# A state-space layer and a top-2 expert layer on one core: expert weights fetched for each slot from DRAM, residual rows in sixteen transfers, blank rows moved ahead of the expert regions

## The reference

```
logits = xf @ Wr + br; top 2 of 16 experts, softmax weights
for each expert e:  h = silu(xf @ W1[e]) * (xf @ W3[e]);  y = h @ W2[e]
                    y = layernorm(y) * gamma[e] + beta[e];  out += weight * y
x = x + layernorm(out)
```

## Time and profile before

| | us |
|---|---|
| median of 3 runs (lowest, highest) | 968.94 (967.91, 969.12) |
| the profiled execution's own time | 968.34 |
| its span in the trace | 966.5 |
| PE busy | 933.1 (97%) |
| DVE, ACT, POOL busy | 724.8, 688.3, 621.8 |
| DMA moved | 75.25 MB |

### The profile page before, as it was taken

The page is one execution under the profiler, slowest core; times in us unless marked ns, Lnnn a source line. Parts: engine busy times, 40 slices in busy tenths (PEclk is TensorE's granted clock), DMA queues, the critical chain, the costliest instruction groups (busy, mean ns, idle before and its releaser), DMA issues.

```text
span 966.5 us, 26600 instructions
## 1 busy us (share of the span) xinstructions
PE 933.1 (97%) x7177; PEld 826.0 (85%) x7177; DVE 724.8 (75%) x2524; ACT 688.3 (71%) x1355; POOL 621.8 (64%) x814
## 2 busy tenths in 40 slices
PE   7999999999999999998959999999999999999995
PEld 4777877888878877887949999999999999999962
DVE  2379999999999998898823777677677677777747
ACT  3777787777788787775215778777777777877626
POOL 2445677777777777775661666666666666576647
PEclk9999999999999999999979999999999999999998
DMA  4001322121111111101786211111111111121076
GB/s 137 12 12 34 93 95 84 58 73 54 56 57 50 56 40 42 40 23 42 263 311 192 69 50 49 46 52 51 44 50 50 45 50 47 45 53 49 19 274 248
DMA packets 52255, 75.25 MB, mean 78 GB/s; under 512 B 11103, under 2 KB 30689, under 8 KB 51472
## 3 DMA queue, kind: packets, MB, share of 16 engines
q1 hardware_dynamic: 41632, 54.61, 18.4%
q0 software_dynamic: 8672, 16.93, 5.2%
q10 hardware_dynamic: 1808, 2.02, 0.7%
HBM read 47.09 MB, written 27.41 MB: 77 GB/s over the span
## 4 chain that ended last, share of the span: by engine, by line
PE 79%; DVE 8%; POOL 6%; issue 5%; DMA 1%; ACT 1%; POOLq 0%; DVEq 0%; SPq 0%; ACTq 0%
PE pA L2106 11%; PE pR L2106 11%; PE pA L1665 11%; PE pB L2114 6%; PE pY L2114 5%; PE pY L1779 4%; PE pB L1691 3%; PE pB L1825 3%; PE pA L1680 3%; PE pY L1815 3%; POOL chosen_scratch L698 2%; PE pY L1798 2%; PE pY L1747 2%; PE pA L1636 2%; PE pR L1763 2%
## 5 line engine op out<-in xcount | busy, mean ns | idle before, releaser
L698 POOL DMA_INDIRECT chosen_scratch<-yo,got_id x143 | 148.2, 1036 | 93.7 <-issue 87.9
L1026 ACT ACTIVATE stage<-w_sb 128x1024 f32 x143 | 151.3, 1058 | 56.6 <-issue 56.5
L1545 DVE TENSOR_TENSOR hidT<-pR,sil 128x512 f32<-128x512 f32 x143 | 98.9, 692 | 80.1 <-ACT sil L1021 59.2
L612 POOL DMA_INDIRECT slots_scratch<-xrow,send_at x128 | 134.6, 1052 | 34.1 <-issue 31.2
L2106 PE MATMUL pA<-xsT,stage 128*128 128x128 f32 x1144 | 151.3, 275 | 0.4 <-ACT xsT L1010 0.4
L2106 PE MATMUL pR<-xsT,stage 128*128 128x128 f32 x1144 | 151.1, 275 | 0.0
L2106 PEld LDWEIGHTS pA<-xsT,stage 128*128 128x128 f32 x1144 | 139.2, 192 | 0.7 <-ACT xsT L1010 0.6
L2106 PEld LDWEIGHTS pR<-xsT,stage 128*128 128x128 f32 x1144 | 139.0, 192 | 0.0
L1665 PE MATMUL pA<-xn,taps 128*128 128x512 f32 x256 | 129.8, 593 | 1.0 <-ACT xn L763 1.0
L688 POOL TENSOR_TENSOR ers<-eve,neg_half 128x1 f32<-128x1 f32 x143 | 81.5, 570 | 57.3 <-DVE eve L1557 32.2
L1021 ACT ACTIVATE sil<-pA 128x512 f32<-128x512 f32 x143 | 85.3, 596 | 25.3 <-PE pA L2106 15.3
(11 more groups left out here) (233 smaller groups left out, 2099.1 us busy)
## 6 DMA issues: line engine op xcount, KB each, us to landing
got<-slots_scratch SPq DMA_DIRECT2D x143, 65.0 KB, 1.8
w_sb<-chosen_scratch SPq DMA_DIRECT2D x16, 512.0 KB, 5.4
w_sb<-in_w_dram SPq DMA_DIRECT2D x1, 6144.0 KB
xin<-in_x_dram SPq DMA_DIRECT2D x16, 256.0 KB
xr<-in_x_dram SPq DMA_DIRECT2D x16, 256.0 KB
x_scratch<-x SPq DMA_DIRECT2D x16, 256.0 KB
w_sb<-in_w_dram SPq DMA_DIRECT2D x4, 1024.0 KB, 8.2
fx<-x_scratch SPq DMA_DIRECT2D x1, 4096.0 KB
```

The source lines that it names most:

```text
L612: eng.indirect_dma_start(slots_d, bass.IndirectOffsetOnAxis(ap=send_at[:, s % 2, k, t:t + 1], axis=0), xrow[:, s % 2, k, t, :], None).then ...
L698: eng.indirect_dma_start(chosen_d, bass.IndirectOffsetOnAxis(ap=got_id[:, j % NGOT:j % NGOT + 1], axis=0), yo[:, q, :], None, bounds_check ...
L1026: eng.activation(stage[:, j % NSTAGE, :, :].rearrange("p k f -> p (k f)"), w13_sb[:, bass.ds(e, 1), :, :].rearrange("p o k f -> p (o k f)" ...
L1545: eng.tensor_tensor(hidT[:, p, :], pR[:, p, :], sil[:, p, :], ALU.mult).then_inc(hid_ready, 1)
```

## The change

- `w13_sb` is no longer filled with weights. SP fetches each slot's 512 KB from DRAM straight into one of the four buffers `stage` (`load_weights`: a register load of the expert's number, a wait for `h3_mm` from slot 4 on, the DMA). The order on SP is slot rows and weights in turn for slots 0 to 3, then the rows of slots 4 to 7, and from then on in each turn n first the weights of slot n-4, then the waits for slot n-8, then the rows of slot n. ACT's `put_weights` is gone.
- Each region now begins with 128 blank rows, written for all 16 regions by one DMA of 1 MB early in stage 1; the tokens' rows start behind them. The tails are gone, with `tail_at`. The first row of a slot is the smaller of its place in the count and 128 rows before the region's end. So the last tile of a region may read rows that the tile before has read as well, or blank rows ahead of the region.
- Two stores that follow each other can therefore write the same rows of `chosen_scratch`; POOL waits before each store until the one before it has landed.
- DVE's table chain has more operations.
- The first layer's result comes back in 16 loads of 256 KB, one in every fourth slot from slot 16 on, and not in one of 4 MB.

```diff
@@ sync @@
-            def load_early():
-                eng.wait_ge(taps_ready, 1)
-                eng.wait_ge(xb_ready, NS)
-                eng.wait_ge(cv_mm, 2 * NS)
-                eng.wait_ge(in_mm, 2 * NS)
-                load_w13(0, 4)
             def load_late():
                 eng.wait_ge(y_step, 11 * NS)
-                load_w13(4, NE)
                 for k, v in enumerate((gamma, beta)):
...
             load_x(5)
+            eng.dma_start(slots_d[0:BLANK, :].rearrange("(e r) d -> e r d", e=NE)[:, 0:P, :].rearrange("e (p r) d -> p e (r d)", r=8),
+                          blank[:, :].rearrange("p (o f) -> p o f", o=1).broadcast_to([P // 8, NE, 8 * ROW])).then_inc(blank_stored, 16)
...
-            load_early()
             store_x1(14)
             load_late()
             store_x1(15)
-            eng.wait_ge(tail_ready, 1)
-            for e in range(0, NE, 2):
-                store_tail(eng, e)
...
-            eng.wait_ge(tails_stored, 16 * NE)
-            eng.wait_ge(blank_stored, 16)
+            eng.wait_ge(blank_stored, 32)
...
+            def load_weights(j):
+                e = eng.value_load(slot_table[0:1, j:j + 1], min_val=0, max_val=NE - 1)
+                wait_past(eng, h3_mm, j - NSTAGE + 1)
+                eng.dma_start(stage[:, j % NSTAGE, :, :], w13[:, bass.ds(e, 1), :, :].rearrange("p o k f -> p (o k) f")).then_inc(staged[j % NSTAGE], 16)
             for j in range(NGOT):
                 load_slots(j)
-            eng.dma_start(fx1[:, :, :, :], x1_d.rearrange("(g p t) d -> p g t d", p=P, t=NT4)).then_inc(fx1_loaded, 16)
-            for n in range(NGOT, NSLOT):
+                if j < NSTAGE:
+                    load_weights(j)
+            for n in range(NGOT, NSLOT + NGOT - NSTAGE):
+                load_weights(n - NGOT + NSTAGE)
+                if n >= NSLOT:
+                    continue
+                if n % 4 == 0 and 4 <= n // 4 < 4 + NG:
+                    g = n // 4 - 4
+                    eng.dma_start(fx1[:, g, :, :], x1_d[g * NT4 * P:(g + 1) * NT4 * P, :].rearrange("(p t) d -> p t d", t=NT4)).then_inc(fx1_loaded, 16)
                 eng.wait_ge(erw_ready, n - NGOT + 1)
                 eng.wait_ge(id_ready, n - NGOT + 1)
                 eng.wait_ge(wb_ready, n - NGOT + 1)
@@ gpsimd, store @@
                 eng.wait_ge(yo_ready, j + 1)
                 eng.wait_ge(id_ready, j + 1)
+                if j:
+                    eng.wait_ge(stored[(j - 1) % 4], ((j - 1) // 4 + 1) * 16)
@@ scalar @@
-            eng.wait_ge(tail_ready, 1)
-            for e in range(1, NE, 2):
-                store_tail(eng, e)
...
-            def put_weights(j):
...
-                if j + 2 < NSLOT:
-                    put_weights(j + 2)
@@ vector, once at the start @@
+                eng.tensor_scalar(running[:, :], running[:, :], float(P), None, ALU.add).then_inc(lower_ready, 1)
@@ vector, positions and the table @@
-                if s == NS - 1:
-                    eng.wait_ge(rank_read, NS)
-                    eng.tensor_scalar(tail_at[:, :], running[:, :], slot_no[:, 0:1], None, ALU.add).then_inc(tail_ready, 1)
...
-            r.step(eng.tensor_scalar(count_i[:, :], count_i[:, :], P - 1, None, ALU.add))
+            r.link(eng.memset(end_step[:, NE - 1:NE], float(BLANK + P)))
+            r.step(eng.tensor_tensor(end_step[:, 0:NE - 1], running[:, 1:NE], running[:, 0:NE - 1], ALU.subtract))
+            r.link(eng.tensor_tensor(end_step[:, NE - 1:NE], end_step[:, NE - 1:NE], running[:, NE - 1:NE], ALU.subtract))
+            r.step(eng.tensor_scalar(count_i[:, :], count_i[:, :], -1, None, ALU.add))
...
+            r.link(eng.tensor_tensor(past_end[:, :, :], past[:, :, :], end_step[:, :].rearrange("p (o e) -> p o e", o=1).broadcast_to([P, 2, NE]), ALU.mult))
             r.link(eng.tensor_reduce(slot_cols[:, 0:2], past[:, :, :], AX.X, ALU.add))
             r.step(eng.tensor_reduce(slot_cols[:, 2:4], past_step[:, :, :], AX.X, ALU.add))
+            r.link(eng.tensor_reduce(slot_end[:, :], past_end[:, :, :], AX.X, ALU.add))
...
-            eng.tensor_scalar(slot_cols[:, 2:4], slot_cols[:, 2:4], float(BLANK), None, ALU.min).then_inc(cols_ready, 1)
+            r.step(eng.tensor_scalar(slot_end[:, :], slot_end[:, :], running[:, 0:1], None, ALU.add))
+            r.step(eng.scalar_tensor_tensor(out=slot_cols[:, 2:4], in0=slot_cols[:, 2:4], scalar=float(2 * P), in1=slot_end[:, :], op0=ALU.add, op1=ALU.min))
+            eng.tensor_scalar(slot_cols[:, 2:4], slot_cols[:, 2:4], float(-P), None, ALU.add).then_inc(cols_ready, 1)
@@ tensor, up @@
-                    eng.wait_ge(staged, j + 1)
+                    eng.wait_ge(staged[j % NSTAGE], j // NSTAGE * 16 + 16)
```

More of the change, by code:

```diff
@@ L137, in sandwich @@
         ones_e = sb("ones_e", [P, NE])
-        tail_at = sb("tail_at", [P, NE], i32)
+        end_step = sb("end_step", [P, NE])
+        past_end = sb("past_end", [P, 2, NE])
+        slot_end = sb("slot_end", [P, 2])
         past = sb("past", [P, 2, NE])
@@ L322, in sandwich @@
         sum_bank = lambda g: w13_sb[:, 0, 0, :] if g == 0 else (pA, pB, pR, pY)[g % 8 // 2][:, g % 2, :]
-        def store_tail(eng, e):
-            row = eng.value_load(tail_at[0:1, e:e + 1], min_val=0, max_val=BLANK - P)
-            eng.dma_start(slots_d[bass.ds(row, P), :].rearrange("(p r) d -> p (r d)", r=8), blank[:, :]).then_inc(tails_stored, 16)
         blank_ready, blank_stored, e_loaded = sem("blank_ready"), sem("blank_stored"), sem("e_loaded")
         pool_passed, dve_passed = sem("pool_passed"), sem("dve_passed")
-        w13_loaded = sem("w13_loaded")
-        staged = sem("staged")
+        staged = [sem(f"staged{q}") for q in range(NSTAGE)]
         w2_loaded = sem("w2_loaded")
@@ L339, in sandwich @@
         stage1_sp = sem("stage1_sp")
-        tables, tail_ready, tails_stored = sem("tables"), sem("tail_ready"), sem("tails_stored")
+        tables = sem("tables")
         cols_ready, cols_mm, table_ready = sem("cols_ready"), sem("cols_mm"), sem("table_ready")
@@ L405, in load_w2 @@
                 eng.dma_start(w2_sb[:, :, 4 * q:4 * q + 4, :], w2[:, :, 4 * q:4 * q + 4, :]).then_inc(w2_loaded, 16)
-            def load_w13(e0, e1):
-                eng.dma_start(w13_sb[:, e0:e1, :, :], w13[:, e0:e1, :, :]).then_inc(w13_loaded, 16)
             load_x(0)
@@ L504, in _ @@
                 eng.wait_ge(stored[q], len(range(q, NSLOT, 4)) * 16)
-            eng.wait_ge(staged, NSLOT)
             for g in range(NG):
@@ L727, in last_add @@
                 eng.tensor_tensor(fx1[:, g, :, :], fn[:, h % 2, q, :, :], fx1[:, g, :, :], ALU.add).then_inc(f_o, 1)
-            eng.wait_ge(fx1_loaded, 16)
+            eng.wait_ge(fx1_loaded, 16 * NG)
             for h in range(len(PARTS)):
@@ L1021, in silu @@
                 eng.activation(sil[:, p, :], pA[:, p, :], ACT.Silu).then_inc(sil_ready, 1)
-            def put_weights(j):
[L1024 to L1029, removed]
             xst(0, 0)
-            put_weights(1)
             for j in range(NSLOT):
```

## The result

The changed kernel takes 1204.89 us (1203.6 to 1206.68), the kernel before beside it 969.03: a ratio of 1.2438, interval 1.2417 to 1.246. The forecast was 965.6, its range ended at 990, and even R1's higher figure, 1107, is 98 us short.

What follows compares the result with a forecast made beforehand. PE was taken to bound stage 2 at 2.79 us a slot; -7.0 + 2.0 + 0.6 + 0.95 + 0.1 = -3.35 gave 965.0 profiled, so 965.6 us (own range 964.5 to 969.4), with a range of 962.5 to 990.

Steps and rivals of the forecast that it cites:

- R1: Rival at POOL's new wait: stores pace stage 2; 1020 us, or about 1107 behind whole loads; 14 in 100.
- the steady pace: Stage 2, each slot: weights land with 1.2 us spare, POOL's new wait is hidden by 0.24 us; cost 0.
- R2: Rival in stage 2: weights come late in each slot, from a landing of 4.55 us; +24, 990 us; 16 in 100.
- POOL's pause: POOL's one long pause in stage 2 makes `erw` late, so weights may reach PE late; half counted, +0.6 us.
- The turn: Before stage 2: without tails and weight loads the queues stop creeping, slot 0 starts at 509.6, not 516.62; -7.0 us.
- The clock's fall: PE, idle before slot 0, may get its lower clock for the first 5 us of slots; +2.5 us, range only.
- slot 4's weights: First weights of the second round land at 522.1, slot 4 due at 520.1; PE waits once, +2.0 us.
- The end: Last two stores: the second must wait for the first, 2.3 us apart instead of 1.34; +0.95 us.

Runs made afterwards that it cites:

- the wait alone: The kernel before plus one line: POOL waits for the landing of the store before each store; 1087.9 us, ratio 1.1228.
- the weights alone: The kernel before with each slot's weights loaded from DRAM and 16 residual pieces; tails stay, no store waits; 976.58 us, ratio 1.0077.
- half the bytes: The changed kernel with W3 left out of the loads, both products using W1, 256 KB a slot; 1132.86 us, ratio 1.169.
- the wait two back: The changed kernel with slots ordered 0, 72, 1, 73, ... and POOL waiting for the store before last; 975.28 us, ratio 1.0078.
- the warm-up of 14: The changed kernel with reordered slots, POOL waiting for the store before last, weights in SBUF copied by ACT, and keep_warm(14) for keep_warm(40); 963.01 us, ratio 0.9941.

## Why the prediction was wrong

**What held.** PE set the pace before, and ACT's copies cost nothing: taking them out gave no gain in any run. The table matmuls take 1.03 us for a forecast 1.06 (in the other kernels without tails 1.0 to 2.4). SP issues weights 1.9 us after `erw`, as forecast. The 36 weight loads whose landing the trace has take 3.5 to 5.8 us, median 3.9, for bounds of 2.9 and 3.8 at a lone load.

**The step that failed: "the steady pace", cost 0.** It had the wait over "2.3 + some 0.25" after a store's start, hidden by 0.24 us. Three terms of it were off, worth 64, 51 and 120 us.

The first is the 0.25; it is 0.94. I took it from the earlier trace rows, where the store at 919.86 stands 0.24 us behind `yo`. That `yo` belongs to the next store. The register move ahead of a store ends 0.71 to 0.72 us before the store's start wherever the chains above show it, so a store at 919.86 cannot go back to a `yo` that ended at 919.62; its own move is recorded at 919.11. The chain of waits follows what stands next on the engine, and that is not always what an instruction waited for. The rows beside it could have told: in the earlier trace rows POOL is idle for 0.63 and 0.64 us ahead of each store "by issue", though nothing was missing. And the trace of the kernel before had the 0.94 itself, at a send that stands right behind the cast of its addresses:

```profile
476.96 0.98 POOL L612 DMA_INDIRECT slots_scratch<-xrow,send_at  x1 [0.94 <-POOL send_at L602]
```

With 0.94 the sum would have been 2.3 + 0.94 = 3.24 against 2.79, and the wait on the path in every slot: +0.45 x 142 = +64 us even with undisturbed landings, and a kernel that is certainly slower. The point from which R1 decides was a landing of 1.85 us, under the shortest landing of the trace (2.1), and not of 2.54.

The second is the median taken for the mean. As long as nobody waits for a store, a late one is free. In the loop each counts: in the run with the wait alone the mean pace is 3.62 for a median of 3.26, 0.36 x 142 = +51 us, which with the 64 make 115 of its 119. The stores behind a fetch are 0.31 of the 0.36 (29 of 125, each 1.35 us late).

The third is the landing itself under the weights' bytes: 3.5 in the mean (median 3.7) for 2.3. I argued against it by the phase: weights 3.5 to 5 us after `erw`, a store at 2.2 to 2.9. That argument failed at its own pace: in the weights alone, at 2.79, the stores' packets end as late as in the changed kernel. There the weights are issued when I said, but their packets run from 0.95 to 3.4 us behind the issue (medians), so from 2.9 to 5.3 after `erw`: a stretch of 2.5 us in every 2.79. It ends 0.3 us after the store's first packets are due, and the slot rows, behind the weights in SP's queue, now run beside the store (median 1.9 us after its start, for 1.3 before). In the changed kernel `erw` and with it SP's issue hang on the store, and the bytes fall at 0.3 to 2.7 us after the next store's start; that changes the phase, not the size of the delay. In the loop it is paid: 4.46 - 3.62, x 142 = +120.

So R1 was the case, at 14 in 100, and the mechanism is as it was put; its higher price, a pace of 3.79, was too small by the 0.69 us of the first term (3.79 + 0.69 = 4.48, measured 4.46). The Trainium skill ("DMA: Bandwidth & Descriptors", section "Queues, rings and completion order") was quoted there for engines that serve their queues in turn, so that a store meets a load's whole share. By that rule landings would be 2.3 + 1.24 = 3.54, and 2.3 + 0.62 = 2.92 at half the bytes; the runs have 3.7 and 2.9 in the median and 3.5 and 3.0 in the mean, so the traces agree with its size. Not each store stands behind the whole load, though: in the changed kernel the last packet of 23 of the 143 ends within 2.1 us of the store's start, as if alone.

**R2** has its own run: 8 us for the 24 forecast. Its pace of 2.79 stayed; what it costs are single late slots, most of all after POOL's pause, for which I had set 0.6 and which takes some 4 us there (two slots of 5.63 and 3.71, from one transpose to the next).

**The turn**, -7.0, gave -3.4 in this trace; with the same turn, slot 0 begins at 513.99 at half the bytes and at 510.73 with the wait two back, so a single trace is good to some 3 us here. Neither the 8 MB of loads nor the tails are what makes the queues creep. With the tails kept and the loads gone (the weights alone) PE's steps end at 505.66, for 504.67 before; with both gone they end at 503.18. In the four traces with tails they end between 504.19 and 505.66, and in six of the seven without between 502.93 and 504.12 (in the seventh, the warm-up of 14, at 506.42), so a part of the tails of 1 to 2 us is likely, and not shown. What holds the queue back for the rest is open. The sends of POOL run in these 8 us in all kernels; they were not tried. That the warm-up then sets the start is shown, by the runs that shorten it. The clock's fall, which I had put behind the warm-up, came within it, for the same 2.5 us: 25 records at 0.57 take 5.0 us and not 2.6. For slot 4's weights (+2.0) no gap of PE shows: issued at 519.70 and landed at 523.4, they were there when slot 4 began at 523.74.

**The end**: the last two stores stand 4.03 us apart for a forecast 2.3, the same error of 0.94 with a landing of 3.1. The fixed 2 us that the prediction quoted there from the Trainium skill ("DMA: Bandwidth & Descriptors", section "Anatomy of one DMA") agree in their size with the 2.3 of a lone store, but not in what they are made of, mostly the write's receipt: 1.6 us pass before the store's first packet starts, 1.03 of them in POOL's instruction, and only 0.35 lie between the end of its last packet and the landing.

## What to carry to other kernels

A wait for the last DMA of the same queue turns a pipeline into a loop, and its time is the landing plus all that its engine does between the landing and the next start; read that from two instructions of which one surely waits for the other, and take the landing's mean, not its median. Before a wait is called hidden, let it wait for the transfer before last and ask what the order of the work must be for that: here it was worth 230 us. A phase between two streams is no argument while one of them fills most of the turn: here the weights' packets took 2.5 us of 2.79, and the stores were late at either pace.

## What the runs showed of the hardware

- An indirect DMA on POOL that waited for a landing starts 0.94 us after it, 0.72 of that behind its register move, with or without other traffic.
- A store of 16 packets of 4 KB lands in 2.3 us alone (1.6 us ahead of its first packet, 0.35 behind its last), and in 2.9 and 3.7 us beside 256 and 512 KB of another queue, which take 0.62 and 1.24 us at 423 GB/s.
- One instruction packet of 16 KB holds up one of a store's 16 packets, and with it the landing of all, by 1.3 us (3.65 for 2.3).
- In stage 2 of the changed kernel PE was busy for 74% and had a granted clock of 0.92 in the mean, against 1.00 when busy throughout: the product records into `pA` take 300 ns for 275.
